# A metaformer block on one core: the convolution stage split from one pass over four images into two passes over pairs of half images

## The reference

```python
x = x + conv_block(ln_over_channels(x))
t = to_tokens(x)                    # 4096 tokens of 128 values
t = t + moe_ffn(ln_over_features(t))
x = from_tokens(t)

def conv_block(x):
    xd = relu(group_norm(conv1x1(x, 128 -> 32)))
    for w, d in zip((wa, wb, wc, wd), (1, 4, 8, 12)):       # four dilations
        f = softmax(conv3x3(xd, w, dilation=d), over 9 filters)
        outs.append(sum(shift(xd, tap k of dilation d) * f[:, k] for k in range(9)))
    y = relu(group_norm(conv1x1(cat(xd, outs), 160 -> 32)))
    return relu(group_norm(conv1x1(y, 32 -> 128)))

def moe_ffn(x):                      # 8 experts, hidden size 512, two best experts per token
    return sum(softmaxed_gate[e] * (gelu(x @ w1[e].T + b1[e]) @ w2[e].T + b2[e]) for e in top2)
```

## Time and profile before

| | us |
|---|---|
| median of 3 runs | 347.08 (345.46 to 347.09) |
| span of the profiled execution (first to last instruction) | 344.3 |
| median less span | 2.8 |
| products, first to last | 38.2 to 104.0 |
| first layer of the first expert step | 155.2 |
| first gather of the second half | 181.6 |
| last scatter issued | 320.1 |

### The profile page before, as it was taken

The page is one execution under the profiler, slowest core; times in us unless marked ns, Lnnn a source line. Parts: engine busy times, 40 slices in busy tenths (PEclk is TensorE's granted clock), DMA queues, the critical chain, the costliest instruction groups (busy, mean ns, idle before and its releaser), DMA issues.

```text
span 344.3 us, 4697 instructions
## 1 busy us (share of the span) xinstructions
PE 290.1 (84%) x1475; PEld 204.3 (59%) x1475; DVE 180.4 (52%) x431; ACT 148.6 (43%) x352; POOL 201.7 (59%) x193
## 2 busy tenths in 40 slices
PE   3999979997999395737999999999999999993054
PEld 0235525352343185616898888888888888882032
DVE  3573597999894778588937111221112222312086
ACT  2562212121102668357756655554554454343082
POOL 9300269787880012077757777777777777775271
PEclk9999998995799989568999999999999999998555
DMA  7100000000000003538434555665666566631585
GB/s 299 63 0 3 0 2 0 0 2 0 0 0 4 0 0 123 185 113 285 154 108 149 182 176 173 201 208 179 177 210 198 177 182 203 198 116 38 207 350 190
DMA packets 13767, 41.79 MB, mean 121 GB/s; under 512 B 3120, under 2 KB 3120, under 8 KB 13744
## 3 DMA queue, kind: packets, MB, share of 16 engines
q1 hardware_dynamic: 8640, 29.52, 25.7%
q0 software_dynamic: 4096, 8.40, 8.1%
q10 hardware_dynamic: 1008, 3.59, 2.6%
HBM read 32.05 MB, written 9.44 MB: 121 GB/s over the span
## 4 chain that ended last, share of the span: by engine, by line
PE 68%; DVE 16%; ACT 6%; DMA 5%; issue 3%; POOL 1%; DVEq 0%; SPq 0%; POOLq 0%; ACTq 0%
PE PS L1398 20%; PE PS L1409 20%; PE PS L1262 6%; PE PS L1248 4%; PE PS L1209 4%; DVE PRF L860 3%; DMA X<-x 3%; PE PS L1326 2%; DVE PRF L1164 2%; PE PS L1365 2%; PE PS L1387 2%; PE PS L1420 2%; ACT SCR L658 2%; DMA SCR<-expert_rows 1%; PE PS L1189 1%
## 5 line engine op out<-in xcount | busy, mean ns | idle before, releaser
L693 ACT ACTIVATE MV<-PS,WE 128x256 f32<-128x256 f32 x156 | 61.1, 474 | 57.3 <-PE PS L1398 57.3
L517 POOL DMA_INDIRECT expert_rows<-RX,dsti x64 | 62.6, 978 | 22.1 <-issue 17.4
L1398 PE MATMUL PS<-SCR,WE 128*128 (+1 forms) x312 | 75.2, 385 | 0.0
L1409 PE MATMUL PS<-MV,WE 128*128 128x256 f32 x312 | 73.8, 379 | 0.0
L472 POOL TENSOR_TENSOR PRF<-PRF 128x1024 f32<-128x1024 f32 x21 | 49.5, 2361 | 41.3 <-DVE PRF L860 39.8
L1409 PEld LDWEIGHTS PS<-MV,WE 128*128 128x128 f32 x312 | 59.0, 190 | 7.7
L1398 PEld LDWEIGHTS PS<-SCR,WE 128*128 128x128 f32 x312 | 57.3, 194 | 6.7 <-issue 0.2
L510 POOL DMA_INDIRECT RX<-token_rows,dsti x46 | 45.1, 981 | 17.3 <-issue 17.3
L1124 DVE TENSOR_SCALAR PRF<-PS,WE 128x256 f32 x30 | 14.5, 484 | 69.3 <-PE PS L1409 68.8
L860 DVE TENSOR_TENSOR PRF<-RX,PS 128x512 f32<-128x512 f32 x66 | 41.8, 677 | 6.8 <-PE PS L1248 6.7
L1248 PE MATMUL PS<-FT,k 72*128 72x512 f16 x72 | 28.7, 427 | 4.0 <-DVE PRF L860 2.5
(11 more groups left out here) (245 smaller groups left out, 386.0 us busy)
## 6 DMA issues: line engine op xcount, KB each, us to landing
WE<-experts SPq DMA_DIRECT2D x39, 514.5 KB, 3.6
token_rows<-SCR SPq DMA_DIRECT2D x4, 512.0 KB, 4.3
SCR<-expert_rows SPq DMA_DIRECT2D x4, 512.0 KB, 8.1
SCR<-expert_rows ACTq DMA_DIRECT2D x4, 512.0 KB, 8.4
out<-PRF SPq DMA_DIRECT2D x8, 256.0 KB, 2.2
X<-x ACTq DMA_DIRECT2D x2, 512.0 KB, 6.2
X<-x SPq DMA_DIRECT2D x2, 512.0 KB, 8.2
first_token_rows<-SCR SPq DMA_DIRECT2D x2, 512.0 KB, 2.6
```

Of the source, the lines that this page charges most:

```text
L517: nc.gpsimd.indirect_dma_start(yr, bass.IndirectOffsetOnAxis(ap=dsti[:, 1, q:q + 1].bitcast(U32), axis=0), YS[:, q % NR, :], None).then_in ...
L693: last = nc.scalar.activation(GF[:, j % 2, c * STEP:(c + 1) * STEP], first_layer(j, c), ACT.Gelu, bias=part(j, "b1")[:, c:c + 1])
L1398: last = nc.tensor.matmul(first_layer(j, c), part(j, "w1")[:, c * P:(c + 1) * P], columns, start=True, stop=True)
L1409: last = nc.tensor.matmul(second_layer(j), part(j, "w2")[:, c * C:(c + 1) * C], GF[:, j % 2, c * STEP:(c + 1) * STEP], start=(c == 0), sto ...
```

## The change

The convolution runs twice, for images 0 and 1 and then for images 2 and 3. A partition now stands for (half h of the picture, image i of the pair, channel), so a product of 128 x 512 covers a whole pair. The planes have 16 rows of their own and 12 rows of padding on either side; the rows that belong to the other half are fetched by a matmul with a permutation (`other`), and group means are made common to both halves by a matmul with `halves`. There are 8 turns (`ND2`: 2 pairs x 4 dilations) of 9 products, 72 products as before, one spread matmul for each as before. The softmax runs on 128 x 144 eight times instead of 128 x 288 four times. POOL sums 43 products of 128 x 512 (21 of 128 x 1024 before) and DVE adds 8 of its own (4 of double width before). The first pair's second normalization, third convolution, third normalization (its sums now on ACT), residual sum, tokens and token statistics are written into the loop of the second pair's products; the same pieces of the second pair are written among the first half's routing and the first expert steps.

```diff
-        PLAN = ('SsDssEsss', 'SsDssEsss', 'SsDssEsss', 'SPsPsDsPE')
-        NPR = ND * KK
+        PLAN = ('SsDssEsss', 'SsDssEsss', 'SsDssEsss', 'SsDssEsPP', 'SsDssEsss', 'SsDssEsss', 'SsDssEsss', 'SPsPsDsPE')
+        NPR = ND2 * KK
...
-        ONES_AT = {2: (0,), 3: (1, 2, 3)}
-        ONE_HOTS_AT = {3: (0,)}
-        ONE_HOTS_EARLY_AT = {4: (1, 2, 3)}
+        ONES_AT = {5: (0, 1), 6: (2, 3)}
+        ONE_HOTS_AT = {7: (0, 1, 2, 3)}
+        TOKENS_AT = {0: (4, 5), 1: (6, 7)}
+        SCALE_AT = 1
+        NORM_AT = {2: (2,), 3: (3,)}
+        RANKS_AT = 3
...
@@ gpsimd
-            pool.wait_ge(logit_done, ND)
-            nc.gpsimd.tensor_copy(IOTA_R, k16_("iota").unsqueeze(2).to_broadcast([P, P, RUN])).then_inc(wide_done, 1)
-            for b in range(B // 2):
-                token_variance(b)
...
@@ scalar, in the expert steps
+                for g in TOKENS_AT.get(j, ()):
+                    evacuate_tokens(1, g)
+                if j == SCALE_AT:
+                    nc.scalar.preload_act_table_set("natural_log_exp_and_others")
+                    token_scale(1)
+                    nc.scalar.preload_act_table_set("gelu_and_others")
+                for b in NORM_AT.get(j, ()):
+                    token_norm(b)
+                    store_rows(b)
...
@@ vector
+            def group_sums(u, p, source):
...
+                chain(nc.vector.bn_stats(st[:, p, u, :], source))
+                chain(nc.vector.bn_aggr(a[:, 0:2], st[:, p, u, :]))
+                chain(nc.vector.tensor_scalar(a[:, 1:2], a[:, 1:2], GN_EPS, None, ALU.add))
+                nc.vector.scalar_tensor_tensor(a[:, 1:2], a[:, 0:1], a[:, 0:1], a[:, 1:2], ALU.mult,
+                                               ALU.add).then_inc(gsum_done, 1)
...
+            def split_plane(p, rows):
...
+                chain(nc.vector.tensor_scalar(XP[p][0][upper[0]], XD[p][upper[0]], SX, None, ALU.mult))
                 for i in range(2):
...
+                    nc.vector.scalar_tensor_tensor(XP[p][i][lower[i]], XD[p][upper[i]], SX, XP[p][i][upper[i]], ALU.mult,
                                                    ALU.subtract).then_inc(xl_done, 1)
...
+            def residual(p, i):
                 for h in range(2):
...
+                    s = pixels(p, i, h)
+                    dve.wait_ge(r3_done, 4 * p + 2 * i + h + 1)
+                    nc.vector.tensor_tensor(X[:, s], X[:, s], R3[:, i, h * HALF:(h + 1) * HALF], ALU.add).then_inc(x1_done, 1)
+
+            def token_sums(p, g):
+                dve.wait_ge(tokc_done, PT * p + g + 1)
+                for t in range(p * HT + 2 * g, p * HT + 2 * g + 2):
+                    nc.vector.bn_stats(st4[:, t, :], XTL[:, t, 0:C]).then_inc(tstat_done, 1)
...
+            FIRST_PAIR_AT = {
+                39: lambda: group_sums(1, 0, bank(ACC_BANK)), 41: lambda: group_variance(1, 0, MID_BANK[0]),
+                42: lambda: group_affine(1, 0), 56: lambda: third_variance(0),
+                58: lambda: third_affine(0), 60: lambda: residual(0, 0), 62: lambda: residual(0, 1)}
+
+            for n in range(NPR):
+                d, k = n // KK, n % KK
+                for ahead_, step in (SOFTMAX_AT if d else FIRST_SOFTMAX_AT).get(k, ()):
+                    if d + ahead_ < ND2:
+                        softmax(d + ahead_, step)
+                product(n)
+                if n == 11:
+                    split_plane(1, NEAR)
+                if n == 13:
+                    split_plane(1, FAR)
+                if n in FIRST_PAIR_AT:
+                    FIRST_PAIR_AT[n]()
+                if 64 <= n < 64 + PT:
+                    token_sums(0, n - 64)
...
+            third_variance(1)
+            destinations(1, PS[:, LOGIT_BANK, STEP:2 * STEP], 0, QA)
+            third_affine(1)
+            for i in range(2):
+                residual(1, i)
+            for g in range(PT):
+                token_sums(1, g)
+            token_variance(1)
+            token_shift(1)
             choose(HT, TT)
             mark(HT, TT)
...
@@ tensor
+            means(0)
+            squared_means(0)
+            first_conv(0)
+            means(1)
+            other_half(0)
+            group_mean(0, 0, FRONT_BANK[0][0])
+            squared_means(1)
+            first_conv(1)
             pe.wait_ge(c16_in, 16)
-            keep_busy(30, 6)
+            keep_busy(8, LOGIT_BANK)
...
+                if 62 <= g < 62 + PT:
+                    tokens(0, g - 62)
...
                 if j < NJ:
                     hidden(j)
...
+                if j == RANKS_AT:
+                    ranks()
+                for g in TOKENS_AT.get(j, ()):
+                    tokens(1, g)
```

968 lines of the change are left out of this document (515 added, 453 removed).

## The result

The changed kernel takes 382.69 us (median of 4 runs, 379.66 to 383.23) against 346.27 for the kernel before in the same measurement; the ratio is 1.112, with a 95% interval of 1.103 to 1.121. The direction was forecast, the size was not: 358.0 was predicted, and the range ended at 368. The profiled execution has a span of 380.2.

What follows compares the result with a forecast made beforehand. DVE was taken as nearly full in the product loop, POOL's transfers as setting the end after the second half's first gather. Stretches 36 + 80 + 33.5 + 46 + 135.5 + 24.2 = 355.2, plus 2.8, gave 358.0 us; range 345 to 368.

Steps and rivals of the forecast that it cites:

- B: The product loop: 80 us (72 to 88) against 65.8 before, with DVE busy 76.0 and 4 idle.
- The three signs: The forecast fails if the loop is shorter than 70, the one-hot products stand before 183, or POOL's pause shrinks.
- The third rival: PE's clock stays at its lower level through the front and the product loop: sum 370, slower, chance 0.06.
- The second rival: The product loop doesn't grow, taking 67 us: total 345.0; chance 0.13, of it 0.08 faster and 0.05 the same.
- The first rival: Experts are not tied to POOL, so the last step ends 157.5 after the first layer: total 341.3, chance 0.08.
- A: From the start to the first product: 36.2 us (33 to 40) against 38.2 before.
- C: From the last product to the first expert layer: 33.5 us (32 to 36) against 51.2 before.
- D: From the first expert layer to the second half's first gather: 46 us (42 to 49) against 26.4 before.
- the chain on PE: After the first expert layer, PE's steps, waits, tokens and table loads put the one-hot matmuls at 38.6 us.
- The other chain, over DVE: After the first expert layer, last tokens, statistics, choice of experts and ranks put the last one-hot rows at 34.3 us.
- E: POOL's transfer list from the second half's first gather: 135.5 us against 138.4 before, its one wait of 2.93 gone.
- The table loads: ACT's two loads ahead of the second expert step's gelu cost 2.6 us; 5.3 by the skill page's added drain.

## Why the prediction missed

**The step that failed is B.** The prediction put DVE at 76.0 and its idle time at 4. DVE was busy 82.66 and idle 13. The upper end of B had the busy time right, by stretching the new pieces 1.5 times (82.6); with its 4.9 of idle time B would have been 87.6, inside 72 to 88. So it is the idle time, which no end of the range let grow, that carried B past it. The three signs that were to show the forecast failing look for a shorter loop, earlier one-hot products and a shorter pause; none of them asked for a loop longer than forecast.

*DVE's busy time, 6.7 over.* The prediction priced the new pieces by rows in which POOL stood still: the residual sums at 2.70, the second plane's split at 3.3, eleven small operations at 2.1. They measured 5.4, 6.1 and 5.5. The contention was seen, in the earlier trace rows, but left to the upper end. What was overlooked is its form: an operation of DVE with both sources in SBUF that meets a running POOL sum is done only behind that sum, on one or two columns 0.02 us behind it, on 144 columns 0.17, on 512 columns 0.55. So a one-column operation loses as much as a wide one. Small operations are therefore the dearest to put there for what they do, and the prediction counted them as the cheapest. An estimate of 5 us was put beside the sum for the contention, by the Trainium skill, "GPSIMD Engine Reference", sections 1 and 8; the run without POOL's sums gives 12.3 us of DVE's time and 9.3 of the loop. The form stands on another page of the Trainium skill, "SBUF — State Buffer", section SBUF: two separate sides: the shared pair of ports is an exclusive lock for a whole instruction, and the other engine blocks. The trace agrees (1.25 us beside a sum of 1.26).

*DVE's idle time, 9 over.* The sentence "PE gains 28 narrow matmuls and a dozen others, of a kind that the loop holds already; it is not the last there unless its clock falls" is where the price was lost. PE gained 20.8 us of busy time, 8.4 of it logit matmuls that had stood ahead of the loop and that the prediction does not name, and 18 us of length by itself. The cover that the prediction assumed is gone: PE at 70.8 and DVE at 82.7 share three banks, and wherever PE has a burst or DVE a held operation, the other waits. Neither alone is the loop: without POOL's sums DVE is busy 70.4 and PE takes 70.8 by itself, and the loop is 86.3. The sums handed to PE show that work added to PE comes back as DVE's waiting (3.1 us more for 2.2 less of busy time). The fillers show that 3 us of the idle time is the clock. How the rest divides between PE's amount of work and the order of its stream is not settled: the two runs with less accumulation, with and without fillers, had a lower granted clock (0.65 and 0.74).

**The third rival was half right.** PE's clock was low in places, but over the loop it was hardly lower than before (0.84 against 0.87), and what it cost there is 3 us, not 8; the fall came behind the loop (0.58 against 0.83) and cost 3 us there. **The second rival** (the loop does not grow) was wrong by 29 us. **The first rival** fell with the tokens ahead of the experts: the experts' start moved by 8 us and the end did not. From the first layer to the transfer that waits for the last step it is 178.0 us, not 157.5, since PE stops for the second half's gather with the first layers of 8 of its 39 steps behind it.

**A** was 1.4 short, which is less than the first product moves from run to run (37.2 to 42.1 in 12 profiles that leave the front as it is). **C** was right in its mechanism and 3.8 short: no clock was put into it. With the clock at 0.98 it takes 34.2. **D**, the later one-hot products, was forecast at 46 and is 47.6, from the chain on PE that was described: they start at 210.32, right behind PE's output layer and 40.0 us after the first expert layer (38.6 forecast), and PE then waits for the gather. The other chain, over DVE, was put 4 us earlier but comes nearly as late: ACT's last copy of the one-hot rows ends only 0.9 us ahead of them. Two rows of the timeline of the kernel after:

```profile
210.32 5.71 PE L1511 MATMUL PS<-PRF,OHR 128*128 128x92 f16 x64
220.56 0.45 PE L1540 MATMUL PS<-prm,RX 128*128 128x128 f32 x1 [4.53 <-DMA RX<-token_rows,dsti]
```

**E** was 2.2 short: the prediction struck out POOL's one wait, and it is there as in the earlier trace rows, in the timeline after, here with PE's first layers behind the gather and in the last step:

```profile
222.14 3.62 PE L1551 MATMUL PS<-SCR,WE 128*128 128x256 f32 x8
...
342.51 1.89 PE L1551 MATMUL PS<-SCR,WE 128*128 x8
...
348.27 0.96 POOL L518 DMA_INDIRECT expert_rows<-RX,dsti  x1 [3.23 <-DVE RX L1264]
```

The prediction set PE's 117 + 6 = 123 us against POOL's 135.5 and left out what stands behind the last step's first layer: 5.8 us to the transfer that waits for it, and 7.3 to the end of the last one. PE takes 4.2 from the gather at 217.94 to its next first layer and 120.4 from there to the last step's, so 137.7 in all; POOL's list without the wait would take 134.7. In all 16 profiles POOL waits here, 2.4 to 3.4 us. From the second half's first gather to the end it is 162.3 us here and 162.7 before, and that the two agree is in part chance: PE had 8 first layers behind it at the gather instead of 5, but then waited for rows and took 4.0 us a step instead of 3.8. **The table loads** took 1.28 us each, and the operation behind the second starts 0.02 after it, as the row of before had said. The rows of ACT in the timeline after:

```profile
185.32 1.28 ACT L791 ACT_TABLE_LOAD   x1
186.62 1.57 ACT L757 ACTIVATE MV<-PS,WE 128x256 f32<-128x256 f32 x4
```

Three slips in the prediction's sums change little: A is 36.2 in its paragraph and 36 in the sum, the last own sum stands in B and again in C, and the lower end of B takes off 5 where its rows give 6.

## What to carry to other kernels

Before work is moved under a loop, make the sum for every engine that the loop uses, with the work that changes sides at the loop's start too: here the moved pieces were priced on DVE, and PE, at nine tenths already, had no room either. Price an operation of DVE with two sources in SBUF that will run beside POOL by what is left of POOL's instruction, not by its own width alone, and keep short chains of tiny operations out of such a stretch. And when much of the work starts only with one result, what counts is when that result is there: the 15 us saved between the loop and the first expert layer were more than lost by the 21 us that came in between that layer and the gather, with the one-hot products three to four steps later. Lastly, let the upper end of a range hold the idle time growing, and not only the busy time.

## What the runs showed of the hardware

- A DVE operation on one column (L898) took 1.25 us beside a POOL sum of 1.26 and 0.21 in the run without POOL's sums; a conversion with a single source in SBUF (L913) took 1.56 beside POOL and 0.44 without. Products with one source in PSUM took 0.67 to 0.68 in both cases, and some operations with a single source in SBUF were not held either: the sums of the softmax (L934) 0.30, its reciprocal (L937) 0.25 and the token statistics (L988) 0.28, in both cases.
- The granted clock over one and the same product loop differed from profile to profile, 0.76 to 0.84 in four of them, and the loop took 95.65 to 98.9. With 50 fillers in it the clock was 0.93 and 0.94 and the loop 92.5 and 91.9. It can also stay low while PE works: in the run with the short accumulations PE was busy 46.33 of the 47 us from 59 to 106 at a granted clock of 0.50.
- 80 fillers took 3.1 us off a stretch of 37.3 (clock 0.58 to 0.98), and 3.4 in the run with both kinds.
- POOL's indirect transfers follow each other at 0.97 us with a pause of 0.30: the 106 behind the gather take 134.7 us without the one wait.
